# Fewer dummy products ahead of six transposes of normalized tokens

## The chip, the cores and the metric

The kernel runs on one core of one Trainium2 chip. The metric is the device time of one execution in microseconds (us); three runs of the kernel before gave 1218.53, 1219.71 and 1220.90 us, a median of 1219.71 us.

## The reference, cut to what matters

128 tokens of 768 numbers in float32 pass through eight layers in turn. Each layer normalizes the tokens and adds its result to them:

```
edge_index = stack([src, dst])
x = x + L0_gnn(layernorm(x))      # 8 heads of 768, hidden width 6144
x = x + L0_ffn(layernorm(x))      # routed tokens get attention, the others a mix; then a small FFN
x = x + L1_gnn(layernorm(x))      # 8 heads of 128
x = x + L1_ffn(layernorm(x))      # 8 experts, top 2, and a shared expert
x = x + L2_gnn(layernorm(x))      # 12 heads of 64
x = x + L2_ffn(layernorm(x))      # 8 small experts, top 2
x = x + L3_gnn(layernorm(x))      # 4 heads of 512
x = x + L3_ffn(layernorm(x))      # 8 experts of width 3072, top 2
```

with `layernorm(x) = (x - mean) / sqrt(var + 1e-5)` over the 768 numbers of a token. The weights, some 430 MB, are read once from HBM.

## The kernel before, in words

There is one program per engine, written out by hand, and they meet through semaphores only. SyncE issues the loads of the weights in one fixed order, in slabs of 128 x 3072 float32 (1.5 MB) into 14 slots (`slab`, line 550); before a load it waits until the slab that had the slot was used. The loads of a mixture's experts (L1_ffn, L3_ffn; `mixture` in SyncE's program) come after the order of the experts is known: SyncE reads it from `sid` (line 584) once VectorE has sorted them (`order_ready`). Loads that need no order (the shared expert of L1_ffn, the first passes of a fixed expert of L3_ffn) are issued before that, as slots come free.

Between two layers the same hand-over happens each time. TensorE's last products leave the new tokens in the PSUM tile AC. VectorE reads the statistics from it (`stats_of_sum`, lines 1007 to 1015) or from SBUF (lines 996 to 998), GpSimd raises the variance to the power -1/2 (`ln_power`, line 647), and VectorE writes the normalized tokens XN in two halves of 384 columns: `tr_half`, then `tr_input` (line 1027; with gain and offset, in L0_ffn, line 1049). TensorE's function `turn` (line 1530) then transposes XN, three blocks of 128 x 128 after each half, into the PSUM tile TP (line 1537); ScalarE copies the two halves to SBUF (`transposed`, line 689; semaphores `tr_early` and `tr_ready`), and TensorE multiplies the next weights by them.

While VectorE and GpSimd work, TensorE has nothing to do. There the program gives it dummy products, identity times identity, whose result nobody reads: `keep_warm(count)` (line 1525). `turn(k, src, warm)` issues `warm` of them before it waits for the first half. Each dummy is a float32 product of 128 x 128 by 128 columns and shows as two matmul instructions, called passes here. TensorE works in the order of its program, so the transposes come behind all the dummies, and a `keep_warm` that stands behind the transposes comes after them.

The eight hand-overs that this document speaks of, by the number k of `turn` and in order of time:

- k=1, into L0_ffn: 32 dummies, and 3 behind the transposes; then the key product (line 2033)
- k=3, inside L0_ffn: 6 dummies
- k=4, into L1_gnn: 15 dummies; then `first_narrow(2)`, whose first products are at line 1584
- k=5, into L1_ffn (`mixture(1)`): 14 dummies, and 4 behind the transposes; then the router's product (line 1804), 10 more dummies and the first pass
- k=6, into L2_gnn: 15 dummies, issued by a `keep_warm` of their own into the PSUM tile PJ; then the product at line 2155
- k=7, into L2_ffn: 15 dummies
- k=8, into L3_gnn: 15 dummies; then `first_narrow(5)`, lines 1556 and 1566
- k=9, into L3_ffn (`mixture(3)`): as k=5

In the two mixtures ScalarE splits the first weights of the second pass (`whole_hi(first + 1, "g")`, line 868, two halves) between its copy of the new tokens (line 695) and `transposed`:

```
                whole_hi(first + 1, "g")
                transposed(k)
```

Of the kernel before, what the change touches and what calls it, by code (L numbers as in the profile page):

```python
# [13 lines left out]
P = 128  # L14
# [266 lines left out]
def gnn_ffn_kernel(nc, x_in, edges_in, weights, rows_in, cols_in, small_in, attn_in, ffn0_vectors, l2_terms_in, out):  # L281
    with ExitStack() as ctx:
# [3 lines left out]
        def psum(name, shape, dt=F32):  # L286
            return ctx.enter_context(nc.psum_tensor(name, shape, dt))
# [3 lines left out]
        def S(name):  # L291
            if name not in sems:
                sems[name] = ctx.enter_context(nc.semaphore(name))
            return sems[name]
# [17 lines left out]
        XN = extra[:, 1, 1 * D:2 * D]  # L312
# [164 lines left out]
        PJ = psum("PJ", [P, 2 * SEG])  # L477
# [1044 lines left out]
        def _(pe):  # L1522
            mm = nc.tensor.matmul

            def keep_warm(count, dst=MS[:, 3 * P:4 * P]):

                for _ in range(count):
                    mm(dst, ident[:], ident[:], start=True, stop=True)  # L1528

            def turn(k, src, warm=0, dst=TP):  # L1530

                keep_warm(warm)
                for half, (given, product) in enumerate((("tr_half", "tr_first"), ("tr_input", "tr_product"))):
                    pe.wait_ge(S(given), k + 1)
                    for t in range(3):
                        at = half * 3 + t
                        ins = nc.tensor.transpose(dst[:, half * SEG + t * P:half * SEG + (t + 1) * P],
                                                  src[:, at * P:(at + 1) * P], ident[:])
                    ins.then_inc(S(product), 1)
# [252 lines left out]
            def mixture(l):  # L1792
                m = MOE[l]
                k, nth = {1: (5, 0), 3: (9, 1)}[l]
                first, end, base = m["first"], LAST_PASS[l], SETS_SO_FAR[l]
                turn(k, XN, warm=14)
                pe.wait_ge(S("x_ready"), {1: 3, 3: 7}[l])
                keep_warm(4)
                pe.wait_ge(S("tr_early"), k)
# [220 lines left out]
            first_wide(0)  # L2020
            second(1, 1)

            turn(1, XN, warm=32)
            keep_warm(3)
            pe.wait_ge(S("tr_early"), 2)
            quarters = [slice(c * BLOCK, (c + 1) * BLOCK) for c in range(4)]
# [109 lines left out]
                mm(AC[:, a:b], FT[0:F0, :], w_tile(31, a, b)[0:F0], start=False, stop=True,  # L2136
                   skip_group_check=True).then_inc(S(name), 1)

            turn(4, XN, warm=15)
            pe.wait_ge(S("tr_early"), 4)  # L2140
            pe.wait_ge(S("x_ready"), 2)
            first_narrow(2)
            second(3, 2)
            mixture(1)

            pe.wait_ge(S("vectors_loaded_0"), 16 * (12 // 2 + 1))
            mm(MS[:, 0:KT * V_COLS], l2_w, l2_a, start=True, stop=True).then_inc(S("l2_v_product"), 1)
            keep_warm(15, PJ[:, 0:P])
            turn(6, XN)
            pe.wait_ge(S("l2_v_ready"), 1)  # L2150
            pe.wait_ge(S("tr_early"), 6)
# [59 lines left out]
                             start=False, stop=(t == 2), skip_group_check=True)  # L2211
                ins.then_inc(S(name), 1)

            turn(8, XN, warm=15)
            pe.wait_ge(S("tr_early"), 8)
            pe.wait_ge(S("x_ready"), 6)
            first_narrow(5)
            second(6, 4)
            mixture(3)

# [116 lines left out]
```

## Time and profile before

| | before |
|---|---|
| median of three runs | 1219.71 us (1218.53 to 1220.90) |
| profiled execution, first to last instruction | 1219.1 us; no other time of it is given, so the span is its own time here |
| TensorE matmul busy | 1153.8 us, 95% of the span |
| VectorE / ScalarE / GpSimd busy | 564.7 / 446.2 / 21.9 us |
| bytes moved by the DMA engines | 443 MB, mean 364 GB/s |
| mean granted TensorE clock | 0.992 |

Busy shares are means over stages with different limits. The profile's 40 slices, of 30.5 us each, tell the stages apart: DMA moves 425 GB/s or nearly so from about 335 to 580 us (the first mixture) and from about 760 us to the end (the second), and 180 to 420 GB/s between these.
### The profile page before, as it was taken

To read this page: it belongs to the slowest core of one execution; us is meant where nothing else is said; L and a number is where in the kernel's file an instruction comes from. 1 tells how busy PE (TensorE), PEld (TensorE's weight loads), DVE (VectorE), ACT (ScalarE), POOL (GpSimd) and SP (SyncE) were. 2 spreads that over 40 slices of the span, in tenths; PEclk is the share of its full clock that TensorE was granted. 3 is DMA by queue.
4 is the path that set the end of the run, shared out by engine and by line. 5 is a ranking of instruction groups with operands and counts; after the bars stand their busy time and mean duration, and the time that the engine had idled before them with its cause. 6 is when DMAs were issued, how large, how long until landed. Compare 5 with 4: busy or idle time off the path is not lost.

```text
span 1219.1 us, 15740 instructions
## 1 busy us (share of the span) xinstructions
PE 1153.8 (95%) x6379; PEld 726.4 (60%) x6379; DVE 564.7 (46%) x880; ACT 446.2 (37%) x516; POOL 21.9 (2%) x47
## 2 busy tenths in 40 slices
PE   5899999989999999989999999999999999889987
PEld 4677786657855455445866786565665555346533
DVE  7977732437644233201665684454554523233410
ACT  4766512215633223201444364343444422222210
POOL 2000000000000000000000000000000000000000
PEclk9999999999999999989999999999999999998999
DMA  9988555945999999999567498999999999999996
GB/s 376 423 364 342 222 208 208 398 182 206 387 417 424 425 425 425 426 420 419 224 239 271 186 396 313 428 425 424 426 426 425 425 425 425 425 425 426 425 423 262
DMA packets 45224, 443.14 MB, mean 364 GB/s; under 512 B 5073, under 2 KB 5233, under 8 KB 11873
## 3 DMA queue, kind: packets, MB, share of 16 engines
q1 hardware_dynamic: 42336, 427.05, 84.7%
q0 software_dynamic: 2816, 15.09, 3.2%
q8 instruction: 51, 0.84, 0.3%
q14 instruction: 21, 0.16, 0.0%
HBM read 441.73 MB, written 0.39 MB: 363 GB/s over the span
## 4 chain that ended last, share of the span: by engine, by line
PE 76%; DMA 12%; DVE 5%; ACT 3%; SPq 2%; issue 1%; POOL 0%; DVEq 0%; ACTq 0%
PE PJ L1896 16%; DMA scratch<-in_weights 11%; PE PJ L1865 10%; PE AC L1933 8%; PE TP L1955 7%; PE PJ L1874 5%; PE AC L1681 3%; PE AC L1693 3%; PE MS L1528 3%; PE PJ L1856 2%; SPq L597 2%; PE TP L1906 2%; PE PJ L1641 1%; DMA ring<-in_weights 1%; PE PJ L1594 1%
## 5 line engine op out<-in xcount | busy, mean ns | idle before, releaser
L1896 PE MATMUL PJ<-scratch,picked 128*64 128x512 f32 (+1 forms) x564 | 146.2, 601 | 2.5 <-DMA scratch<-in_weights 2.5
L1955 PE MATMUL TP<-ring,extra 128*64 128x512 f32 (+3 forms) x720 | 118.0, 488 | 0.0
L1310 DVE TENSOR_TENSOR ring_lo<-ring,w_hi_u 128x1536 fp32r<-128x1536 f32 x46 | 79.6, 1756 | 71.9 <-ACT w_hi_u L868 71.7
L1292 DVE SCALAR_TENSOR_TENSOR act<-low,CB,PJ 128x512 f32<-128x512 f32 x51 | 38.0, 745 | 160.1 <-PE PJ L1865 84.1
L851 ACT ACTIVATE low<-PJ 128x512 f32<-128x512 f32 x51 | 30.2, 592 | 218.9 <-PE PJ L1896 146.3
L1896 PE MATMUL PJ<-ring,picked 128*32 128x512 f32 (+1 forms) x456 | 101.6, 594 | 0.0
L868 ACT ACTIVATE w_hi_u<-ring 128x1536 fp32r<-128x1536 f32 x46 | 66.9, 1484 | 59.7 <-PE AC L1933 27.7
L1310 DVE TENSOR_TENSOR ring_lo<-ring,w_lo_u 128x1536 fp32r<-128x1536 f32 x40 | 68.9, 1755 | 37.4 <-ACT w_lo_u L868 37.4
L1955 PEld LDWEIGHTS TP<-ring,extra 128*64 128x64 f32 (+1 forms) x720 | 46.3, 126 | 60.0 <-issue 51.0
L1874 PE MATMUL PJ<-ring_lo,XTh 128*128 128x512 f32 x198 | 79.0, 399 | 0.0
L1896 PEld LDWEIGHTS PJ<-scratch,picked 128*64 128x64 f32 (+1 forms) x564 | 42.7, 126 | 59.1 <-issue 58.4
L868 ACT ACTIVATE w_lo_u<-scratch 128x1536 fp32r<-128x1536 f32 x32 | 46.8, 1485 | 79.5 <-DMA scratch<-in_weights 55.1
L868 ACT ACTIVATE w_lo_u<-ring 128x1536 fp32r<-128x1536 f32 x40 | 57.8, 1483 | 34.2 <-PE AC L1933 19.0
L1865 PE MATMUL PJ<-w_lo_u,extra_lo 128*128 128x512 f32 x150 | 60.5, 403 | 0.0
L1865 PE MATMUL PJ<-w_hi_u,extra_lo 128*128 128x512 f32 x150 | 58.8, 403 | 1.2 <-DVE ring_lo L1310 1.2
L1933 PE MATMUL AC<-w_hi_u,extra_lo 128*128 128x512 f32 x208 | 50.4, 356 | 9.3 <-DVE extra_lo L1318 9.3
L1865 PE MATMUL PJ<-w_lo_u,XTh 128*128 128x512 f32 x150 | 59.2, 395 | 0.0
L1865 PE MATMUL PJ<-w_hi_u,XTh 128*128 128x512 f32 x150 | 59.2, 394 | 0.0
L1896 PE MATMUL PJ<-extra,picked 128*64 128x512 f32 (+1 forms) x132 | 58.6, 594 | 0.0
L1896 PEld LDWEIGHTS PJ<-ring,picked 128*32 128x32 f32 (+1 forms) x456 | 29.3, 120 | 43.4 <-issue 42.6
L1933 PE MATMUL AC<-w_lo_u,extra_lo 128*128 128x512 f32 x192 | 46.4, 355 | 7.4 <-DVE extra_lo L1318 7.4
L868 ACT ACTIVATE w_hi_u<-scratch 128x1536 fp32r<-128x1536 f32 x20 | 28.7, 1481 | 66.3 <-DMA scratch<-in_weights 64.3
(439 smaller groups left out, 2114.6 us busy)
## 6 DMA issues: line engine op xcount, KB each, us to landing
ring<-in_weights SPq DMA_DIRECT2D x158, 1536.0 KB, 18.6
scratch<-in_weights SPq DMA_DIRECT2D x78, 1536.0 KB, 22.1
extra<-in_weights SPq DMA_DIRECT2D x23, 1536.0 KB, 21.6
extra<-in_attn POOLq DMA_DIRECT2D x11, 768.0 KB, 9.9
ring<-in_weights SPq DMA_DIRECT2D x10, 768.0 KB, 29.1
scratch<-in_weights SPq DMA_DIRECT2D x12, 384.0 KB, 15.9
extra<-in_attn POOLq DMA_DIRECT2D x6, 512.0 KB, 9.2
extra<-in_weights SPq DMA_DIRECT2D x4, 768.0 KB, 25.0
```

Of the source, the lines that this page charges most:

```text
L851: A(silu, PJ[:, 0:SEG], ACT.Silu).then_inc(S("silu_ready"), 1)
L868: A(hi_half(n, half), half_slab(n, half), ACT.Copy).then_inc(S("whole_hi"), 1)
L1292: v.scalar_tensor_tensor(hexp, silu, weight, PJ[:, SEG:2 * SEG], ALU.mult, ALU.mult) \
L1310: v.tensor_tensor(slab_lo(n)[:, half * HALF:(half + 1) * HALF], half_slab(n, half), hi_half(n, half).bitcast(F32), ALU.subtract).then_inc( ...
L1528: mm(dst, ident[:], ident[:], start=True, stop=True)
L1681: ins = mm(AC[:, a:b], act1T[:, j % 2, t * P:(t + 1) * P], slab_at(n)[:, t * D + a:t * D + b], start=(j == 0 and t == 0), stop=(j == last ...
L1693: ins = mm(AC[:, a:b], x[:, t * P:(t + 1) * P], w[:, t % 2 * D + a:t % 2 * D + b], start=(j == 0 and t == 0 and x is xl), stop=False, skip ...
L1865: return mm(dst, x[:, t, :], hi_half(n, t // 3)[:, t % 3 * SEG:(t % 3 + 1) * SEG], start=start, stop=stop)
L1874: mm(dst, XTh[:, t, :], slab_lo(n)[:, t * SEG:(t + 1) * SEG], start=(apart and t == 0), stop=False)
L1896: ins = mm(dst[c], x[:, t, c], slab_at(LOAD[q, kind, side])[:, t * SEG:(t + 1) * SEG], start=(t == 0), stop=(t == KT - 1))
L1933: ins = mm(AC[:, a:b], x[:, t * P:(t + 1) * P], w[:, a:b], start=False, stop=(q == end and t == 3 and w is hi and x is hTh), skip_group_ch ...
L1955: ins = mm(Y[c, a:b], hT_of(q)[:, t * P:(t + 1) * P][:, c], slab_at(LOAD[q, "d", side])[:, t * D + a:t * D + b], start=(j == j0 and t == 0 ...
```

## The change

Six of the hand-overs get fewer dummies; nothing else is changed. The first hunk lies in the function `mixture` and so counts twice (k=5 and k=9).

```diff
-                turn(k, XN, warm=14)
+                turn(k, XN, warm=11)
...
-            turn(1, XN, warm=32)
+            turn(1, XN, warm=17)
...
-            turn(4, XN, warm=15)
+            turn(4, XN, warm=10)
...
-            keep_warm(15, PJ[:, 0:P])
+            keep_warm(10, PJ[:, 0:P])
             turn(6, XN)
...
-            turn(8, XN, warm=15)
+            turn(8, XN, warm=10)
```

That is 3 + 15 + 5 + 5 + 5 + 3 = 36 dummies, or 72 passes, fewer. The hand-overs k=3 and k=7 keep their 6 and 15.

## Rows read from the trace of the kernel before

**Rows 1.** The page of the profile, its head

```profile
span 1219.1 us, 15740 instructions
```

**Rows 2.** Chain that ended last, in order of time (start us, us, what): hand-overs k=1, 4, 5, 6

```profile
167.00 7.14 PE MS L1528 x64
...
222.90 3.54 PE MS L1528 x30
...
274.31 3.12 PE MS L1528 x28
...
571.03 3.35 PE PJ L1528 x30
```

**Rows 3.** Timeline, k=1 (start us, us, engine, line, operation, tiles, count; idle before in brackets)

```profile
170.10 1.15 DVE L1049 SCALAR_TENSOR_TENSOR extra<-extra,rstd,scratch 128x384 f32<-128x384 f32 x2 [0.69 <-POOL rstd L647]
...
173.98 0.82 PE L1537 MATMUL TP<-ident,extra 128*128 128x128 f32 x6
174.51 0.87 ACT L689 ACTIVATE extra<-TP 128x384 f32<-128x384 f32 x2 [6.17 <-PE TP L1537]
174.64 0.83 PE L1528 MATMUL MS<-ident 128*128 128x128 f32 x6
175.31 4.18 PE L2033 MATMUL PJ<-extra,ring 128*128 128x128 f32 x36
```

**Rows 4.** Timeline, hand-overs that the change leaves alone: k=3 (217 us), k=7 (600 us)

```profile
217.34 1.15 DVE L1049 SCALAR_TENSOR_TENSOR extra<-extra,rstd,scratch 128x384 f32<-128x384 f32 x2 [0.51 <-POOL rstd L647]
218.01 1.07 PE L1537 MATMUL TP<-ident,extra 128*128 128x128 f32 x6
...
600.31 0.87 DVE L1027 TENSOR_SCALAR extra<-extra,mv,rstd 128x384 f32<-128x384 f32 x2 [0.68 <-POOL rstd L647]
...
600.84 0.94 PE L1537 MATMUL TP<-ident,extra 128*128 128x128 f32 x6 [0.29 <-DVE extra L1027]
601.43 0.88 ACT L689 ACTIVATE extra<-TP 128x384 f32<-128x384 f32 x2 [5.44 <-PE TP L1537]
```

**Rows 5.** Timeline, k=4

```profile
224.72 0.87 DVE L1027 TENSOR_SCALAR extra<-extra,mv,rstd 128x384 f32<-128x384 f32 x2 [0.66 <-POOL rstd L647]
226.28 0.82 PE L1537 MATMUL TP<-ident,extra 128*128 128x128 f32 x6
226.80 0.87 ACT L689 ACTIVATE extra<-TP 128x384 f32<-128x384 f32 x2 [2.63 <-PE TP L1537]
227.35 1.13 PE L1584 MATMUL PJ<-ring,extra 128*128 128x512 f32 x2 [0.25 <-ACT extra L689]
```

**Rows 6.** Timeline, k=5, the first mixture

```profile
275.47 2.86 ACT L868 ACTIVATE w_hi_u<-scratch 128x1536 fp32r<-128x1536 f32 x2
...
277.27 0.82 PE L1537 MATMUL TP<-ident,extra 128*128 128x128 f32 x6
...
278.21 0.87 ACT L689 ACTIVATE extra<-TP 128x384 f32<-128x384 f32 x2
278.82 1.45 PE L1804 MATMUL MS<-small,extra 128*128 128x8 f32 x12
```

**Rows 7.** Waits of SyncE's queue, whole span (waiter <- releaser: us in all, times, longest)

```profile
SPq L584 <- DVE sid L1336: 41.5, 2, 21.3
```

**Rows 8.** Stretches (us; PE, PEld, DVE, ACT, POOL busy; granted clock; DMA share, GB/s)

```profile
171.00:173.00 2.00, 2.00 (x21) 2.00 (x20) 1.81 (x4) 0.00 (x0) 0.00 (x0) 1.00 0.00 0
...
213.00:222.80 9.80, 9.05 (x46) 5.79 (x45) 4.71 (x9) 2.63 (x4) 1.25 (x1) 1.00 0.85 339
...
286.00:288.00 2.00, 2.00 (x6) 0.86 (x5) 1.76 (x10) 0.00 (x0) 0.00 (x0) 1.00 0.00 0
...
545.00:550.00 5.00, 5.00 (x20) 1.93 (x18) 0.00 (x0) 0.00 (x0) 0.00 (x0) 0.76 1.03 422
```

**Rows 9.** Chain that ended last, in the first mixture, around a wait for a load

```profile
543.69 7.07 PE PJ L1896 x24
...
551.34 5.33 PE PJ L1896 x24
```

## The prediction

> **What bounds the kernel now.** I began with the head of the page: the profiled execution spans 1219.1 us [rows 1], 0.6 us under the median of 1219.71. Next came the chain that ended last, in order of time. In the hand-overs between two layers it runs through the dummies themselves [rows 2]: 64 passes at k=1, 30 at k=4, 28 at k=5, 30 at k=6; k=8 repeats k=6, and k=9 repeats k=5. So at six places dummies stand where something useful could. One pass takes 7.14 us / 64 = 0.112 us, one dummy 0.223 us. The chain can mislead here: with nothing later to point at, it goes back to the instruction before on the same engine. So I read each hand-over's timeline, to see when the tokens were ready and who else had to be ready.
>
> Then I asked whether a gain of a few us in a hand-over lives to the end, since long stages are bound by the loads. The stretches say that no load is under way at 171 to 173 us, nor at 286 to 288 [rows 8]; the same zero stands at 598 to 600, 614 to 618 and 685 to 695 us. SyncE's queue waits 21.3 us at the longest, twice in all, for the sorted experts (`sid`) [rows 7], the last work ahead of each mixture's stream of loads. So the streams have no fixed place in time: each begins when TensorE and VectorE have brought it on, and what comes before it earlier brings the whole stream earlier.
>
> **The change, place by place.** Transposes start behind the last dummy or when the first half of XN is there, whichever is later. Two untouched hand-overs show the second case. At k=7 TensorE has been idle 0.29 us when the half arrives: the transposes start 0.53 us after VectorE's two writes start, and ScalarE's copy 1.12 us after them [rows 4]. At k=3, where the writes are the longer form (line 1049), the transposes start 0.67 us after them and last 1.07 us instead of 0.82.
>
> *k=1, 15 dummies fewer.* 30 passes x 0.112 = 3.35 us. The dummies would end so that the transposes could start at 173.98 - 3.35 = 170.63; the first half comes at 170.10 + 0.67 = 170.77 [rows 3, 4]. So they start at 170.77, 3.21 us earlier. They wait for the second half in between and last 1.07 us in place of 0.82, so that the three dummies behind them and the key product come 3.21 - 0.25 = 2.96 us earlier. I take 2.96. Two other things are late next and do not bind: the key product's weights are there, as the loads had ended by 171 us [rows 8], and ScalarE, whose copies at 174.51 now run about 3.2 us earlier, was idle 6.17 us before them.
>
> *k=4, five fewer.* 10 passes are 1.12 us: start possible at 226.28 - 1.12 = 225.16, tokens there at 224.72 + 0.53 = 225.25. ScalarE's copy then starts at 224.72 + 1.12 = 225.84 instead of 226.80 [rows 4, 5], 0.96 us earlier, and the products behind it as much.
>
> *k=6 and k=8, five fewer each.* The same pattern with the same durations (30 passes in 3.35 us [rows 2], the same two writes); between the start of the writes and that of the transposes lie 1.59 us there, 1.56 at k=4. I take 0.96 us for each.
>
> *k=5 and k=9, three fewer each.* 6 passes are 0.67 us, and the tokens would allow 0.6 of them. But the next link is ScalarE's copy, and ScalarE is still splitting weights: two halves of 2.86 us from 275.47 on, behind which the copy starts at once, at 278.21 [rows 6]. The split does not wait for the transposes. The copy keeps its time, and the router's product can start 0.55 us behind it at the earliest (as line 1584 does at k=4 [rows 5]), at 278.76, as against 278.82: 0.06 us each. The bounds are 0 and the 0.6 us of the transposes; ScalarE's row decides for the lower end. In place of the removed dummies TensorE stands idle for half a us there.
>
> **The sum.** 2.96 + 3 x 0.96 + 2 x 0.06 = 5.96 us off 1219.1 gives 1213.1; with the 0.6 us between the span and the median, 1213.7 us. The ends: all 72 passes come off (8.0 us, 1211.7), or nothing does. No edit adds a wait or a DMA, and none moves a step past another on any queue. Against the gain stands only the restart of TensorE after a short idle time, which the 0.59 us from transposes to copy at k=7 against the 0.52 or 0.53 of the other places [rows 3 to 5] put at 0.07 us; it is in the numbers above. How far it may grow the trace does not show; up to 0.1 us more at each of six places I allow for.
>
> **Whether the clock stays.** The dummies may be there for TensorE's clock. The row nearest to the changed places is the untouched k=3: with 6 dummies, a transposition that waits for both halves and 0.75 us idle in all, the stretch from 213 to 222.8 us was granted 1.00, the 2.4 GHz level [rows 8]. The trace shows the clock lower only after long stalls: in the first mixture, after TensorE had waited 2.5 us for a load, 24 products took 7.07 us where the same 24 took 5.33 a little later [rows 9], and 545 to 550 us was granted 0.76, part of it at 1.2 GHz [rows 8]. With the change no wait before a transposition is over 0.2 us by the numbers above. By these rows the clock stays. The Trainium skill's page "TensorE: Matmul & The Clock Gate", section "Part 4: PE-mode transpose", speaks against the change: transposes do not count as activity for the clock gate in the way that products do, so dummies would hold the clock where transposes don't. By that rule the stretches in question lose counted work, and the sum would be that of the second rival; the 1.00 at k=3 does not agree with it, at least not for so short a stretch.
>
> **The rivals.**
> 1. *The loads end the wait anyway.* If the first mixture's stream of loads keeps its place in time, what is won ahead of it (2.96 + 0.96 + 0.06 = 3.98 us) is spent waiting for loads in that stage, and k=6, 8 and 9 alone count: 1219.71 - 1.98 = 1217.7 us, within 0.2% of before. For it: late in the stage the DMA engines are full (422 GB/s, share 1.03 [rows 8]). Against it: no load is under way ahead of the order [rows 8], and SyncE waits for it [rows 7]. Chance 0.05.
> 2. *The clock falls behind the thinned stretches; slower.* Price: 7.07 - 5.33 = 1.74 us each time [rows 9], at the first real products behind the transposes. At all six, 10.4 us against 5.96 of gain: 1224.1 us. It decides from four places on (6.96 us). For it: without enough work in front, a lower clock was granted [rows 8]. Against it: k=3, and idle times of a tenth of those that were followed by a drop. Chance 0.04.
> 3. *The dummies were cover everywhere.* As at k=5, something not in the chain (the copy, a load, the second half) holds the next product at all six places: 1219.7 us. Rows 3 and 5 show an idle ScalarE ahead of the copy, against it. Chance 0.03.
> 4. *All 72 passes come off*, because the normalized tokens are ready sooner than I read and ScalarE is no bound in the mixtures: 1211.7 us. Against it: rows 4 and 6. Chance 0.04.
>
> **How the numbers follow.** The forecast, 1213.7 us, has the remaining 0.84. Its own spread is that of the three runs, 1.2 us to either side, and the 0.6 us of restarts: 1212.5 to 1215.5. The range takes in the case of all passes and rounds the upper end: 1211.7 to 1216.0, which leaves out rivals 1 to 3 (0.12) and a little of the spread. A change under 0.2% (2.4 us) can hardly be told from none. Faster by more: forecast and rival 4, 0.88. Within: rivals 1 and 3, 0.08. Slower by more: rival 2, 0.04.
>
> **What the next profile would show.** Right: at k=1, 4, 6 and 8 the transposes start 0.5 to 0.7 us after VectorE's writes start, with VectorE named as the releaser; in both mixtures line 689 still starts where line 868 ends, and line 1804 follows TensorE idle time of about 0.5 us; the loads of each mixture start some 4.0 and 6.0 us earlier than before; the clock is 1.00 in the six stretches. Wrong: line 2033 or 1584 waits for a DMA; the clock is below 1.00 in the stretch behind a hand-over; line 689 moves with the dummies in the mixtures; or the early start is lost as a longer wait for loads in the first mixture.

## The result, and the profile after

| | before | after |
|---|---|---|
| median of four runs each | 1220.31 us (1218.53 to 1221.49) | 1214.05 us (1212.21 to 1216.26) |
| profiled execution: span | 1219.1 us | 1213.8 us |
| PE busy | 1153.8 us | 1147.2 us |

The ratio is 0.9948, with an interval from 0.9934 to 0.9961: 6.26 us between the medians, where 5.96 was forecast; the new median lies 0.35 us from the 1213.7 of the forecast and inside its range. So close a hit is in part luck: by the interval the gain is 4.8 to 8.1 us. In the changed kernel's profiled execution the run took 1215.62 us and the span 1213.8, so 1.8 us lie outside the span; the same holds for the other profiled runs below. By that the execution of [rows 1], with its 1219.1 us of span, is the one of 1220.90 us, and the 0.6 us that the prediction put between span and median joined two different executions; its sum, made against 1220.90, gives 1214.9 for the 1215.62 measured.

The gain is made where it was forecast. First the timeline of the changed kernel at k=1, which answers to [rows 3]:

```profile
166.81 3.96 PE L1528 MATMUL MS<-ident 128*128 128x128 f32 x34
...
170.07 1.15 DVE L1049 SCALAR_TENSOR_TENSOR extra<-extra,rstd,scratch 128x384 f32<-128x384 f32 x2 [0.69 <-POOL rstd L647]
...
170.74 1.07 PE L1537 MATMUL TP<-ident,extra 128*128 128x128 f32 x6
171.32 1.02 ACT L689 ACTIVATE extra<-TP 128x384 f32<-128x384 f32 x2 [3.01 <-PE TP L1537]
...
172.32 1.95 PE L2033 MATMUL PJ<-extra,ring 128*128 128x128 f32 x16
```

The transposes now follow VectorE's writes by 0.67 us and last 1.07 us, as at k=3 [rows 4]. Line 2033 starts 5.51 us behind the first dummy (166.81) where it was 8.47: 2.96 us. At k=4, the same view [rows 5]:

```profile
221.74 0.87 DVE L1027 TENSOR_SCALAR extra<-extra,mv,rstd 128x384 f32<-128x384 f32 x2 [0.67 <-POOL rstd L647]
222.27 0.94 PE L1537 MATMUL TP<-ident,extra 128*128 128x128 f32 x6
222.86 0.89 ACT L689 ACTIVATE extra<-TP 128x384 f32<-128x384 f32 x2 [1.67 <-PE TP L1537]
223.40 2.84 PE L1584 MATMUL PJ<-ring,extra 128*128 128x512 f32 x6 [0.19 <-ACT extra L689]
```

0.53 us from the writes to the transposes and 1.12 to the copy, as at k=7 [rows 4]. At k=6 the product behind the transposes stood in the kernel before at

```profile
575.38 1.49 PE L2155 MATMUL MS<-extra 128*128 128x24 f32 x12 [0.35 <-ACT extra L689]
```

4.51 us behind the first dummy (570.87), and in the changed kernel it stands at

```profile
570.78 1.49 PE L2155 MATMUL MS<-extra 128*128 128x24 f32 x12 [0.28 <-ACT extra L689]
```

3.51 us behind the first dummy (567.27). At k=5, to set beside [rows 6]:

```profile
270.19 2.62 PE L1528 MATMUL MS<-ident 128*128 128x128 f32 x22
...
271.51 2.86 ACT L868 ACTIVATE w_hi_u<-scratch 128x1536 fp32r<-128x1536 f32 x2
...
272.73 0.94 PE L1537 MATMUL TP<-ident,extra 128*128 128x128 f32 x6
...
274.26 0.87 ACT L689 ACTIVATE extra<-TP 128x384 f32<-128x384 f32 x2
274.80 1.50 PE L1804 MATMUL MS<-small,extra 128*128 128x8 f32 x12 [0.24 <-ACT extra L689]
```

Here the transposes come earlier, but line 689 still starts where line 868 ends, 1.53 us behind the start of the transposes; TensorE now waits for the copy, and line 1804 has won 0.07 us.

From the first dummy of k=1 on, the span can be cut at such starts. Each row is the time between two of them:

| from the start of | to the start of | before | after | difference |
|---|---|---|---|---|
| first dummy, k=1 | line 2033 | 8.47 | 5.51 | -2.96 |
| line 2033 | line 1584 (contains k=4) | 52.04 | 51.08 | -0.96 |
| line 1584 | line 1804 (contains k=5) | 51.47 | 51.40 | -0.07 |
| line 1804 | first dummy, k=6 (first mixture) | 292.05 | 292.47 | +0.42 |
| first dummy, k=6 | line 2155 | 4.51 | 3.51 | -1.00 |
| line 2155 | first dummy, k=8 (L2) | 42.16 | 43.86 | +1.70 |
| first dummy, k=8 | line 1566 | 4.42 | 3.42 | -1.00 |
| line 1566 | line 1804 of k=9 (contains k=9) | 62.85 | 62.79 | -0.06 |
| line 1804 of k=9 | end (second mixture) | 534.3 | 533.0 | -1.3 |

The six hand-overs give 6.05 us. What the other three rows add, 0.8 us, is in stretches that the change does not touch. The largest is the small FFN of L2. In the kernel before, the six products at line 2210 show as

```profile
612.74 2.84 PE L2210 MATMUL AC<-ring,scratch 128*128 128x512 f32 x6
```

and in the changed one as

```profile
608.15 4.54 PE L2210 MATMUL AC<-ring,scratch 128*128 128x512 f32 x6
```

4.54 - 2.84 = 1.70 us, the whole of that row. The stretches of the changed kernel say why (columns as in [rows 8]):

```profile
605.00:607.00 2.00, 1.32 (x10) 1.11 (x10) 1.96 (x2) 0.65 (x3) 0.00 (x0) 1.00 0.95 362
607.00:609.00 2.00, 1.87 (x3) 0.79 (x4) 1.94 (x2) 0.00 (x0) 0.00 (x0) 0.80 0.89 381
609.00:611.00 2.00, 2.00 (x4) 0.80 (x3) 0.00 (x0) 0.00 (x0) 0.00 (x0) 0.50 0.02 6
```

The granted clock is 0.50, the 1.2 GHz level, for some us. In the six hand-overs it stays at 1.00 (k=1, 4, 5, 6, 8 and 9 in this order):

```profile
170.00:176.00 6.00, 6.00 (x52) 5.61 (x52) 2.71 (x5) 2.56 (x4) 0.79 (x2) 1.00 0.01 3
222.00:228.00 6.00, 5.81 (x21) 2.97 (x20) 0.61 (x2) 0.89 (x2) 0.00 (x0) 1.00 1.01 423
272.00:282.00 10.00, 9.76 (x66) 7.88 (x65) 6.78 (x18) 8.07 (x9) 0.16 (x1) 1.00 0.01 2
567.00:575.00 8.00, 7.72 (x67) 7.31 (x66) 2.15 (x8) 3.41 (x7) 1.13 (x2) 1.00 1.01 423
614.00:622.00 8.00, 7.81 (x47) 6.62 (x46) 2.71 (x7) 1.49 (x5) 0.55 (x1) 1.00 0.51 197
676.00:688.00 12.00, 11.75 (x82) 9.65 (x81) 8.48 (x25) 9.32 (x11) 0.56 (x1) 1.00 0.13 57
```

The streams of loads begin earlier by what was won ahead of them. VectorE's write of the sorted order was in the kernel before

```profile
288.34 0.17 DVE L1336 CAST sid<-r 128x8 int32<-128x8 f32 x1
```

and in the changed kernel's timeline it is

```profile
284.38 0.17 DVE L1336 CAST sid<-r 128x8 int32<-128x8 f32 x1
```

3.96 us earlier, and over the whole span SyncE's queue waits for the sorted orders of the two mixtures as long as before [rows 7]:

```profile
SPq L584 <- DVE sid L1336: 41.5, 2, 21.3
```

### The profile page after: what moved, and what is told of

Read it like the earlier page. It is cut to its first block, busy times and chain, and to the rows that moved or that the text cites. A ratio compares the mean times of both kernels' runs of the same rounds, so it can differ in the third digit from the quotient of the medians.

```text
span 1213.8 us, 15596 instructions
## 1 busy us (share of the span) xinstructions
PE 1147.2 (95%) x6307; PEld 717.6 (59%) x6307; DVE 564.9 (47%) x880; ACT 446.8 (37%) x516; POOL 21.9 (2%) x47
## 4 chain that ended last, share of the span: by engine, by line
PE 75%; DMA 14%; DVE 6%; ACT 4%; issue 1%; SPq 0%; POOL 0%; DVEq 0%; ACTq 0%
PE PJ L1896 15%; PE PJ L1865 10%; PE TP L1955 8%; DMA scratch<-in_weights 7%; PE AC L1933 7%; DMA ring<-in_weights 6%; PE PJ L1874 5%; PE AC L1681 3%; PE AC L1693 3%; PE PJ L1856 2%; PE TP L1906 2%; PE MS L1528 2%; PE PJ L1641 1%; PE TP L1824 1%; DVE extra L1058 1%
```

## The experiments

The theory: at k=1, 4, 6 and 8 the dummies stood between ready tokens and the transposes, at k=5 and 9 they stood beside ScalarE's split; what is won is carried through the streams of loads whole; and the clock holds because the idle time stays short. The rivals of the prediction and a question that the profile raised, the fall of the clock in L2, are what the runs are to decide. Each ratio is to times of the kernel before that were taken alongside.

**The changed kernel again.** No edit.

> The changed kernel once more. Theory (the gain is made in the hand-overs and carried whole): 5.5 to 7 us less than the kernel before, the product at line 2033 starts 2.96 us earlier counted from the first dummy of k=1, and 0.96 to 1.0 us less in each of k=4, 6 and 8. In the first profile of the changed kernel the clock fell to 0.50 at 609 to 611 us, in the small FFN of L2, behind products that the change does not touch, and 1.7 us went there. If that is a matter of chance from execution to execution, this profile may show 1.00 there and then a span 1.7 us shorter (about 1212); if the change causes it, it stands in this profile again.

Measured: 1214.36 us against 1220.66, ratio 0.9945 (0.9927 to 0.9963). The rows of k=1, k=4 and k=5 in the table above came out as 2.96, 0.98 and 0.07 us (k=1 counted from line 1789), those of k=6 and k=8 as 0.99 and 1.00. The clock was 1.00 at 608 to 611 us, but fell at 601 to 605 us, on the product at line 2193, and at 636 to 640 us. So falls between 595 and 645 us do not sit at one instruction. This execution (1217.92 us) spans 1216.2 us and not about 1212: the fall at 609 us was gone, but two others came, and from the sorted order to the dummies of k=6 it took 284.63 us, where the first execution took 282.89.

**Only the two places ahead of the first mixture.**

```diff
-            turn(1, XN, warm=32)
+            turn(1, XN, warm=17)
...
-            turn(4, XN, warm=15)
+            turn(4, XN, warm=10)
```

> Only k=1 (32 to 17 dummies) and k=4 (15 to 10) are changed; both lie ahead of the first mixture. Theory (the stream of loads starts when the order of the experts is there): 2.96 + 0.96 = 3.9 us less than the kernel before, a ratio of 0.9968, and the dummies of k=6 start 3.5 to 4 us earlier than at 570.87. Rival (the loads end the wait anyway): the dummies of k=6 start at 570.9 as before, and the time is that of the kernel before within 0.5 us.

Measured: ratio 0.9964 (0.9952 to 0.9977), which holds the 0.9968 of the theory and excludes the 1.0 of the rival. Its timeline has

```profile
284.61 0.17 DVE L1336 CAST sid<-r 128x8 int32<-128x8 f32 x1
```

which is 3.73 us earlier than 288.34 (the execution was 0.2 us later at k=1 already). The dummies of k=6 start at 567.96, 2.91 us earlier and not 3.5 to 4. The first mixture, from the sorted order to there, took 282.53 us before, 282.89 in the changed kernel and 283.35 here; a spread of this size between executions is what the gain has to be seen through. The gain is not spent there: the first rival falls.

**14 dummies in the mixtures again.**

```diff
-                turn(k, XN, warm=11)
+                turn(k, XN, warm=14)
```

> The changed kernel with 14 dummies again at k=5 and k=9 (11 in the changed one). Theory (ScalarE's split is what the router's product waits for): from the first dummy of k=5 to the start of line 1804 4.68 us as before, against 4.61 with 11, so 0.07 us apart, and ScalarE's line 689 starts in both where line 868 ends; the time is that of the changed kernel. Rival (the dummies are on the path here too): line 1804 starts 0.6 us later than with 11, in both mixtures, and the time is 1.2 us longer.

One execution, 1217.40 us; a single time does not tell 1.2 us from none, so the starts have to decide. From the timeline at k=5:

```profile
270.23 3.29 PE L1528 MATMUL MS<-ident 128*128 128x128 f32 x28
271.55 2.86 ACT L868 ACTIVATE w_hi_u<-scratch 128x1536 fp32r<-128x1536 f32 x2
...
274.30 0.87 ACT L689 ACTIVATE extra<-TP 128x384 f32<-128x384 f32 x2
...
274.90 1.45 PE L1804 MATMUL MS<-small,extra 128*128 128x8 f32 x12
```

From the first dummy to line 1804 are 4.67 us with 14 and 4.61 with 11, and line 689 starts 2.75 us behind line 868 in both; at k=9 the first distance is 4.67 and 4.61 as well. Three dummies are worth 0.06 us there, not 0.6.

**No dummies at the six places.**

```diff
-                turn(k, XN, warm=11)
+                turn(k, XN, warm=0)
...
-            turn(1, XN, warm=17)
+            turn(1, XN, warm=0)
...
-            turn(4, XN, warm=10)
+            turn(4, XN, warm=0)
...
-            keep_warm(10, PJ[:, 0:P])
             turn(6, XN)
...
-            turn(8, XN, warm=10)
+            turn(8, XN, warm=0)
```

> All six hand-overs with no dummies ahead of the transposes. By the theory of the waits the transposes are bound by the tokens already, so nothing more is won: the starts of the transposes and the products behind them stay as in the changed kernel. What is open is the clock: TensorE then stands idle for 2.4 us at k=4, 6, 8, 2.5 at k=5 and 9 and 4 us at k=1. If the clock stays, the time is that of the changed kernel, 6 us below the kernel before. If it falls, the granted clock behind the transposes is 0.5 for some us at each such place, with about 1.7 us lost where it happens (24 products took 7.07 in place of 5.33 us): with four to six of them 1 to 4 us slower than the kernel before.

Measured: 1227.81 us, ratio 1.0048 (1.0033 to 1.0063) to the kernel before: 7 us slower than it, more than expected, and 13 slower than the changed kernel. At k=1 its timeline (TensorE alone) reads

```profile
171.53 1.43 PE L1537 MATMUL TP<-ident,extra 128*128 128x128 f32 x6 [3.77 <-DVE extra L1049]
172.76 1.49 PE L1528 MATMUL MS<-ident 128*128 128x128 f32 x6
174.04 4.81 PE L2033 MATMUL PJ<-extra,ring 128*128 128x128 f32 x36
```

and its stretches

```profile
172.00:174.00 2.00, 2.00 (x10) 1.94 (x10) 1.56 (x4) 1.47 (x3) 0.00 (x0) 0.50 0.00 0
...
226.00:228.00 2.00, 2.00 (x4) 0.89 (x4) 0.00 (x0) 0.52 (x2) 0.00 (x0) 0.50 0.97 393
...
284.00:286.00 2.00, 2.00 (x11) 2.00 (x11) 1.73 (x10) 1.98 (x2) 0.00 (x0) 0.50 0.00 0
```

The transposes start as long behind the last products of the layer (line 1789, 166.20) as in the changed kernel, 5.33 us, so the waits say the same; but after 3.77 us of idle time the clock is at 0.50, and line 2033 comes 0.93 us later than there. From line 2033 to line 1584 it takes 52.04 us in place of 51.08, and from there to line 1804 54.03 in place of 51.40. The clock is low for some 3 us behind k=1, 7 at k=4 and 10 at k=5 (278 to 288 us, TensorE busy all the time); why it stays low longer at one place than at another is not shown. Counted from line 1789 the sorted order (293.27) comes 8.10 us later than in the changed kernel, 2.7 us for each of the three places. The clock fell behind k=6 and k=8 too; behind k=9, after 2.37 us of idle time, it did not:

```profile
690.00:694.00 4.00, 1.83 (x14) 1.56 (x14) 3.16 (x7) 3.89 (x6) 0.56 (x1) 1.00 0.22 92
```

and it is 1.00 on to 700 us. The twelve executions of this version were granted 0.980 on the mean, the ten of the changed kernel 0.991. That is 0.011 of 1226 us, 13 us of work at full clock by this estimate, as much as was lost. The second rival is a true mechanism, and against it the dummies help.

**Five fewer still at each place** (k=1 12; k=4, 6, 8 five; k=5, 9 six).

```diff
-                turn(k, XN, warm=11)
+                turn(k, XN, warm=6)
...
-            turn(1, XN, warm=17)
+            turn(1, XN, warm=12)
...
-            turn(4, XN, warm=10)
+            turn(4, XN, warm=5)
...
-            keep_warm(10, PJ[:, 0:P])
+            keep_warm(5, PJ[:, 0:P])
...
-            turn(8, XN, warm=10)
+            turn(8, XN, warm=5)
```

> Five more dummies taken from each of the six places (k=1 12, k=4, 6 and 8 5 each, k=5 and 9 6 each), so that TensorE is idle for about 1.1 us ahead of each transposition. The waits say that nothing is won: the transposes stay bound by the tokens. If the clock bears 1.1 us of idle time, the time is that of the changed kernel, ratio 0.995 to the kernel before. If not, the granted clock falls behind some of the six and each costs 0.9 to 2.6 us as in the run with none: ratio 0.998 to 1.005.

Measured: ratio 0.9966 (0.9950 to 0.9983), between the two cases. In the profiled execution nothing is won at k=1, 4 and 5 (the three distances are those of the changed kernel to 0.03 us) and the clock stays there, but behind k=6 it falls:

```profile
570.62 0.94 PE L1537 MATMUL TP<-ident,extra 128*128 128x128 f32 x6 [1.02 <-DVE extra L1027]
```

```profile
574.00:576.00 2.00, 2.00 (x11) 2.00 (x10) 0.00 (x0) 0.85 (x1) 0.20 (x1) 0.50 1.07 444
```

The first fence is its timeline at k=6, with 1.02 us idle ahead of the transposes, the second a stretch behind it. From line 2155 to line 2188 are 28.43 us in place of 26.79. At the other five places the idle time is as long, 1.02 to 1.09 us, and no fall follows. So 1.0 us of idle time is mostly borne. Whether it brought on the one fall is not shown: some 30 us further on the clock falls without it in other traces. Whether this version is slower than the changed kernel on the whole its interval does not decide; nothing shows it faster.

**The kernel before, a second trace.** No edit.

> The kernel before once more, for its trace alone. The first profile of it has a granted clock of 1.00 from 548 to 1042 us; four profiles of kernels with fewer dummies have one or two falls to 0.50 between 600 and 640 us, also the one in which k=6 and k=8 kept their 15 dummies. If these falls are chance from execution to execution, this profile may show one between 595 and 645 us too, and a second look without one would leave it open. If the change makes them, the clock is 1.00 there again.

One execution, 1220.15 us. Stretches:

```profile
602.00:604.00 2.00, 1.86 (x14) 1.78 (x14) 0.02 (x1) 2.00 (x4) 0.00 (x0) 1.00 0.00 0
604.00:606.00 2.00, 2.00 (x5) 1.11 (x5) 1.76 (x9) 2.00 (x2) 0.00 (x0) 0.64 0.00 0
606.00:608.00 2.00, 2.00 (x5) 1.08 (x4) 2.00 (x2) 1.98 (x3) 0.00 (x0) 0.51 0.00 0
```

The clock falls in L2 in the unchanged kernel too, so the change is not needed for it. Its two traces have none and one such fall, those of the kernels with fewer dummies one or two; whether the change makes them more frequent so few traces cannot say. Over the whole span it does not make the mean clock lower: the 48 executions of the kernel before and the ten of the changed one were granted 0.991 alike, and one fall of 3.4 us would take 0.0014 off. By this estimate the change adds less than one fall to an execution; where the falls lie the means do not tell.

**Dummies where TensorE idles in L2.**

```diff
-            turn(7, XN, warm=15)
+            turn(7, XN, warm=17)
...
             add_tokens(start=True)
+            keep_warm(4, TP[:, 2 * SEG:2 * SEG + P])
             pe.wait_ge(S("l2_weighted"), 1)
...
                     if 0 <= t - 1 < n:
+                        if n == 4 and t == 2:
+                            keep_warm(4)
                         term_rows(c, t - 1)
```

> The changed kernel with dummies added where TensorE idles between 595 and 640 us: k=7 17 in place of 15, 4 ahead of the wait for the weighted hidden values in the small FFN of L2 (0.85 us idle there), 4 ahead of the second term rows of L3_gnn (0.8 us idle). If the falls of the clock there come from these idle times, the clock is 1.00 from 590 to 645 us and the time 0.5 to 2 us under the changed kernel, about 0.9935 of the kernel before. If they come from the small products as such, it falls there as before and the time is that of the changed kernel, 0.995.

Measured: ratio 0.9950 (0.9935 to 0.9965), the changed kernel's. In its trace the clock falls at 599 to 603 us, behind k=7 and ahead of the other two places:

```profile
598.00:600.00 2.00, 2.00 (x6) 1.21 (x6) 1.76 (x9) 2.00 (x2) 0.00 (x0) 0.82 0.00 0
600.00:602.00 2.00, 2.00 (x4) 1.01 (x3) 2.00 (x2) 1.98 (x3) 0.00 (x0) 0.50 0.00 0
```

From 594 us to there TensorE was idle for 0.19 us in all. So idle time of the kind that was filled is not what it takes. This trace has no fall at the two other filled places, but neither has the first trace of the kernel before; what does make the clock fall in L2 stays open.

**The mixtures' waits opened.** Lines behind the edit move by one: 1804 is 1805 in this trace.

```diff
-                whole_hi(first + 1, "g")
+                whole_hi(first + 1, "g", (0,))
                 transposed(k)
...
-                whole_hi(first + 1, "u", (0,))
+                whole_hi(first + 1, "g", (1,))
                 act.wait_ge(S("router_shifted"), nth + 1)
...
-                whole_hi(first + 1, "u", (1,))
+                whole_hi(first + 1, "u")
...
-                whole_lo(first + 1, "g")
+                whole_lo(first + 1, "g", (0,))
                 dve.wait_ge(S("router_product"), nth + 1)
...
                 sort(WORLDS[l][0])
+                whole_lo(first + 1, "g", (1,))
                 whole_lo(first + 1, "u")
...
-                keep_warm(4)
+                keep_warm(2)
                 pe.wait_ge(S("tr_early"), k)
...
-                keep_warm(10, PJ[:, 0:P])
+                keep_warm(2, PJ[:, 0:P])
```

> The changed kernel, with the two mixtures' waits opened: ScalarE splits one half ahead of its copy of the tokens and the other behind it, VectorE takes the second half's rest after the sort, and TensorE has 2 dummies in place of 4 ahead of the router's product and 2 in place of 10 behind it. Theory (the router's product waits for ScalarE, the order of the experts for TensorE, and the stream of loads for the order): line 1804 starts 0.5 to 0.9 us earlier counted from the first dummy of k=5, the sorted order is there about 2 us earlier in each mixture, and the time is 2 to 4 us under the changed kernel, 0.992 to 0.9935 of the kernel before. Rival: the first pass or a later split holds TensorE anyway and the loads are late by as much: within 0.5 us of the changed kernel.

Measured: 1210.12 us against 1219.80, ratio 0.9923 (0.9906 to 0.9939), the fastest of all. Timeline at k=5:

```profile
271.47 1.49 ACT L868 ACTIVATE w_hi_u<-scratch 128x1536 fp32r<-128x1536 f32 x1
...
273.27 0.88 ACT L689 ACTIVATE extra<-TP 128x384 f32<-128x384 f32 x2 [0.31 <-PE TP L1538]
273.90 1.42 PE L1805 MATMUL MS<-small,extra 128*128 128x8 f32 x12
...
281.86 0.17 DVE L1336 CAST sid<-r 128x8 int32<-128x8 f32 x1
```

ScalarE's copy now waits for the transposes, where it had waited for the split; the router's product starts 3.75 us behind the first dummy in place of 4.61 (what the divided split and what the two dummies fewer have of this is not parted), and the sorted order comes 13.11 us behind the layer's last products (268.75) where it was 15.59: 2.48 us, and 2.74 at k=9. That is 5.2 us earlier; the time is about 3 us under the changed kernel by the two ratios (0.0025 of 1220). Whether the rest is lost in the streams or in the spread the runs do not settle.

**Only the dummies behind the router's product.**

```diff
-                keep_warm(10, PJ[:, 0:P])
+                keep_warm(2, PJ[:, 0:P])
```

> The changed kernel with only the 10 dummies behind the router's product cut to 2, in both mixtures; ScalarE and VectorE as they were. It parts what the run with the opened waits won. Theory: 8 dummies are 1.79 us on TensorE's way to the count of the chosen, and VectorE's choice is ready 1.6 to 2 us ahead of it, so the sorted order comes 1.6 to 1.8 us earlier in each mixture, counted from the first dummy of the hand-over, and the time is 2.5 to 3.5 us under the changed kernel: 0.992 to 0.9935 of the kernel before. The rest, up to 0.9 us in each mixture, was the order of ScalarE's split. Rival: it was the split alone; then the order comes no earlier and the ratio is that of the changed kernel, 0.995.

Measured: 1212.47 us against 1220.90, ratio 0.9929 (0.9917 to 0.9940). In the second mixture the order comes 12.70 us behind the layer's last products, in place of 14.50, the 1.8 us expected. In the first the profiled execution shows nothing won (15.48 in place of 15.59), and why:

```profile
276.00:278.00 2.00, 2.00 (x10) 1.67 (x10) 1.59 (x7) 2.00 (x3) 0.00 (x0) 0.66 0.00 0
278.00:280.00 2.00, 2.00 (x4) 0.74 (x3) 1.48 (x8) 1.98 (x2) 0.00 (x0) 0.50 0.00 0
```

The clock fell just there and took back 1.7 us. By the mean of 0.66 it fell at about 276.65 us, when TensorE had begun the four passes that this version keeps:

```profile
276.48 1.10 PE L1528 MATMUL PJ<-ident 128*128 128x128 f32 x4
```

Up to there this kernel does what the changed kernel does, instruction by instruction, and TensorE had been idle for 0.24 us in the last five. So the dummies that are missing here cannot have brought the fall on: in the changed kernel too the clock can fall at k=5, though its own two traces show 1.00 there. Of the four traces that are the changed kernel up to this place one has the fall, of the four with 14 dummies at k=5 none has it, nor has the one with six. Whether the three dummies fewer matter there these traces do not show.

The rival, that the split was all, falls with the second mixture. Between this version and the one with the waits opened the times do not decide: their intervals overlap.

## Why the prediction was right

- *The dummies at k=1, 4, 6 and 8 are on the path.* 2.96, 0.96, 1.00 and 1.00 us, against 2.96 and three times 0.96. The 0.04 us more at k=6 are nearly all the 0.03 us by which the writes lay further ahead there (1.59 us against 1.56), which the prediction had read and left out. The two hand-overs that the change leaves alone had shown the time from VectorE's writes to the transposes (0.67 and 0.53 us) to 0.01 us.
- *The mixtures' dummies are not*, although the chain of waits runs through them [rows 2]: 0.07 and 0.06 us against 0.06. The run with 14 of them shows it, and the run with the split divided agrees that the wait was for ScalarE. Of the half us of idle time forecast ahead of line 1804 the trace shows 0.24.
- *The streams of loads follow.* The order was there 3.96 us earlier at k=5, where 3.98 were forecast, and the run with only the early places kept the gain. At k=9 it came 3.89 us earlier in the profiled executions, not 6: of the 6.0 won up to there, 0.42 went in the first mixture and 1.70 in L2, neither at a place that the change touches. The second mixture then took 1.3 us less, which no run explains; the forecast of 6 us there did not come true in this pair.
- *No clock fell at the changed places* in the two traces of the changed kernel, as forecast. It was less safe than the prediction took it: with only the dummies behind the router's product trimmed, a fall began at k=5 where the two kernels are still the same. The rival is real: with no dummies it makes the kernel slower than before, and with 1.0 us of idle time at each place a fall was seen behind one of the six. The prediction priced it at 1.74 us a place; with no dummies the three places ahead of the first order cost 2.7 us each, because the clock stayed low there for up to 10 us.
- *Wrong was a sentence beside the sum*: that the clock falls only after long stalls. It had one trace to go by, in which 2.2 to 3.4 us of idle time lie ahead of each fall; the second trace of the same kernel shows a fall at 605 us with no idle time over 0.3 us ahead of it.
- The third and fourth rivals fall with the table: neither nothing nor all 72 passes came off.

The Trainium skill's page "TensorE: Matmul & The Clock Gate", section "Part 1: The HAM clock gate (the "warmup" mystery)", says that the throttled clock is the default and activity releases it. The run with no dummies agrees: 0.50 behind 3.77 us of idle time. That transposes count less as activity than products, no run here shows apart from the idle time ahead of them.

## What to carry to other kernels

Count filler work so that it ends when the awaited data comes: read the two starts from the timeline, divide the difference by the duration of one filler, and take off that many and no more. A chain of waits that names filler proves nothing by itself; look which engine the next real step waits for. And before a few us in a short stage are believed in, look whether the long stage behind it starts at a fixed time or at an event of that stage.

## What the runs showed of the hardware

- Leaving out the run with no dummies, nine of ten traces have a fall of the granted clock to 0.50, for 3 to 4 us, between 595 and 645 us, the unchanged kernel's second trace among them. A fall there cost up to 1.7 us. The idle time of TensorE in the five us ahead of these falls was 0.19 to 1.12 us in all, and it does not foretell them: 0.19 us went ahead of one, while 1.0 us at once was borne at five places of six in another trace, and 2.37 us at k=9 in the run with no dummies.
- Executions of one kernel differ by 4 us (1212.2 to 1216.3 us for the changed one). Between its two traces the spans differ by 2.4 us, and 1.7 us of that lies in the first mixture, behind the sorted order; why is not shown.
